# Grouping the depthwise tap rounds of layer 1: six groups of three in place of twelve groups of one or two

## What is computed

```
y = einsum(w_in (288x48), x)                      # 48 -> 288 channels
f = rfft2(8x8 patches of y) * fft_mask; y = irfft2(f)
y = conv 3x3 depthwise (288 channels, padding 1)  # nine taps
x1, x2 = split(y, 2)
out = einsum(w_out (48x144), gelu(x1) * x2);  x = x + out
```

## Time and profile before

| | before |
|---|---|
| median of three runs | 21097.66 us (21091.03 to 21103.62) |
| the profiled execution, own time | 21103.45 us |
| its span | 21101.9 us |
| PE busy, mean granted clock | 90%, 0.955 |
| DVE, ACT, POOL busy | 64%, 36%, 49% |

### The profile page before, as it was taken

The page is one execution under the profiler, slowest core; times in us unless marked ns, Lnnn a source line. Parts: engine busy times, 40 slices in busy tenths (PEclk is TensorE's granted clock), DMA queues, the critical chain, the costliest instruction groups (busy, mean ns, idle before and its releaser), DMA issues. The chain is left out here.

```text
span 21101.9 us, 501412 instructions
## 1 busy us (share of the span) xinstructions
PE 19033.5 (90%) x172464; PEld 11794.6 (56%) x172464; DVE 13401.1 (64%) x22319; ACT 7503.4 (36%) x22720; POOL 10333.9 (49%) x8692
## 2 busy tenths in 40 slices
PE   6998998989989989899899898999998989898999
PEld 4665455456655554566555445665555456565666
DVE  4444445656667776666677766666777667777744
ACT  3554232145542221455422214663222122222222
POOL 0000000067767740677677406886774078787810
PEclk9999999999999999999999999999999999999999
DMA  3231112655533336455333364553434666666633
GB/s 92 68 70 45 35 36 84 140 112 113 113 99 111 110 119 145 109 112 113 99 110 111 112 151 111 121 121 100 111 110 126 134 146 150 149 149 146 147 88 78
DMA packets 932423, 2318.18 MB, mean 110 GB/s; under 512 B 276340, under 2 KB 528504, under 8 KB 844124
## 3 DMA queue, kind: packets, MB, share of 16 engines
q1 hardware_dynamic: 500560, 1364.68, 27.8%
q0 software_dynamic: 430080, 928.96, 16.7%
HBM read 1915.53 MB, written 385.13 MB: 109 GB/s over the span
## 5 line engine op out<-in xcount | busy, mean ns | idle before, releaser
L1840 POOL DMA_INDIRECT e_got<-table,e_idx x6144 | 7479.2, 1217 | 2580.1 <-issue 1603.5
L1856 POOL DMA_INDIRECT e_got<-table,e_idx x2048 | 2553.1, 1247 | 691.6 <-issue 501.7
L1010 PE MATMUL b_p_conv<-b_z,b_diag 32*32 32x512 f32 x76032 | 2807.1, 599 | 3.3 <-issue 3.3
L530 PE MATMUL a_p_qk<-a_wst,a_stack 125*128 125x192 f32 x12288 | 2466.8, 337 | 230.9 <-ACT a_qh L661 214.0
L530 PEld LDWEIGHTS a_p_qk<-a_wst,a_stack 125*128 125x128 f32 x12288 | 2025.8, 191 | 670.5 <-issue 367.5
L1112 ACT ACTIVATE b_z<-b_p_z 128x256 f32<-128x256 f32 x2112 | 846.5, 401 | 4026.9 <-PE b_p_z L974 3608.2
L1894 DVE TENSOR_TENSOR e_got<-e_got,e_wt 128x1536 f32<-128x1536 f32 x1024 | 1778.6, 1752 | 684.9 <-DMA e_got<-table,e_idx 682.3
L1199 DVE TENSOR_TENSOR b_ym<-b_p_in,b_mask 128x512 f32<-128x512 f32 x1056 | 729.4, 691 | 1807.8 <-PE b_p_in L966 1807.6
L974 PEld LDWEIGHTS b_p_z<-const,b_ym 128*128 128x128 f32 x8448 | 1165.3, 198 | 1215.5 <-issue 713.3
L974 PE MATMUL b_p_z<-const,b_ym 128*128 128x128 f32 x8448 | 1541.1, 307 | 100.1 <-ACT b_z L1112 93.9
L2140 PE MATMUL d_p_v<-d_xs,d_ws 125*128 125x512 f32 x4608 | 1388.2, 449 | 64.0 <-issue 60.4
(11 more groups left out here) (291 smaller groups left out, 35444.6 us busy)
## 6 DMA issues: line engine op xcount, KB each, us to landing
e_got<-table,e_idx POOLq DMA_INDIRECT x8192
b_x<-planes SPq DMA_DIRECT2D x264, 395.1 KB
a_stack<-in_xp SPq DMA_DIRECT2D x256, 387.0 KB
c_stack<-planes SPq DMA_DIRECT2D x256, 387.0 KB
d_stack<-planes SPq DMA_DIRECT2D x512, 193.5 KB
table<-i_acc SPq DMA_DIRECT2D x256, 384.0 KB, 2.3
b_xr<-planes SPq DMA_DIRECT2D x264, 197.5 KB
planes<-b_out SPq DMA_DIRECT2D x264, 197.5 KB
```

Of the source, the lines that this page charges most:

```text
L530: m = pe.matmul(dst_, st[:, row, dx + 128 * t:dx + 128 * t + 128], wst[:, dx, 0:2 * C2], start=(dx == 0), stop=False)
L1010: mm = pe.matmul(p_conv[q // 2 * 2 + r % 2][BLK * c:BLK * (c + 1), :], diag[g][BLK * r:BLK * (r + 1), k, :], zs[BLK * r:BLK * (r + 1), g, ...
L1840: pool.indirect_dma_start(out=self.got[q][:, t, c * REC:(c + 1) * REC], out_offset=None, in_=self.flat, in_offset=bass.IndirectOffsetOnAxi ...
L1856: pool.indirect_dma_start(out=self.got[q][:, t, c * REC:(c + 1) * REC], out_offset=None, in_=self.flat, in_offset=bass.IndirectOffsetOnAxi ...
```

## The change

The eighteen rounds of a step stand in groups of three at slots 3, 5, 7 (g = 0) and 10, 12, 14 (g = 1). Before, they stood at slots 3 to 8 and 10 to 15 as 2, 1, 2, 1, 2, 1 for each g. No round, copy or product is added or taken away. `gelu(m, 0)` and `gates(m, ., 0)` stand one slot earlier. The number of beats per step stays at 16 from taps.

```diff
-    CONV = {3: (0, 0, 2), 4: (0, 2, 3), 5: (0, 3, 5), 6: (0, 5, 6), 7: (0, 6, 8), 8: (0, 8, 9),
-            10: (1, 0, 2), 11: (1, 2, 3), 12: (1, 3, 5), 13: (1, 5, 6), 14: (1, 6, 8), 15: (1, 8, 9)}
+    CONV = {3: (0, 0, 3), 5: (0, 3, 6), 7: (0, 6, 9), 10: (1, 0, 3), 12: (1, 3, 6), 14: (1, 6, 9)}
...
-                            taps(m, z[1 - par], *CONV[t], (2 if t in (3, 7, 10, 14) else 1) if half else 0)
+                            taps(m, z[1 - par], *CONV[t], (2 if t in (7, 14) else 3) if half else 0)
...
-                        if mid and t == 9:
+                        if mid and t == 8:
                             gelu(m, 0)
...
-                        if mid and t == 9:
+                        if mid and t == 8:
                             gates(m, 1 - par, 0)
```

## The result

The changed kernel takes **21507.36 us** (median of four runs, 21485.39 to 21514.08), the kernel before 21094.35 us in the same comparison (21084.56 to 21103.62). The ratio is 1.0193, with a 95% interval from 1.0178 to 1.0208: 413 us slower. The profiled execution has a span of 21499.5 us, 398 above that of before. 21500 was forecast.

What follows compares the result with a forecast made beforehand. PE was taken to bound layer 1, waits included. Steps without a jump at +3.5 us (19 an image) and with one at +2.7 (13) gave +406 us for four images, forecast 21500 us; own range 21400 to 21610, 8 in 10 21380 to 21660.

Steps and rivals of the forecast that it cites:

- The two waits: PE waits for ScalarE's `b_z` copy four times a step, 0.6 us each; `widen` for `xf` or `xp`, 0.4 to 0.6.
- even slots, `z` uncovered: Slots 4, 6, 8: without the single round, the next inverse waits for ScalarE's copy; +0.65 us each, +2.05 a step with gelu.
- odd slots, `xf` uncovered: Slots 11, 13, 15: without the single round, `widen` waits for ScalarE's `xf` copy; +0.55 us each, +1.65 a step.
- the jump: End of a loop iteration, thirteen steps an image: the `xf` wait vanishes in PE's idle time and `widen` starts earlier, -0.25 us.
- the rounds: Tap rounds on PE: six groups of three at 3.35 us replace six pairs and six singles, -0.2 us a step.
- The extra 0.1 for the moved gelu: Slot 8: `gelu(m, 0)` stands ahead of the copy on ScalarE and delays it, 0.1 us.
- three rounds are dear: Rival, chance 0.1: a group of three takes 3.53 us, +1.2 a step against the sum, +154, giving 21655 us.
- About 3.6 in place of 4.1: Loop jump: fewer us of "issue" per jump, counted as PE's idle time, about 3.6 in place of 4.1.
- Fewer switches: Rival, chance 0.05: with copies ready in time, each tap group removed saves up to 0.2 us; -179, giving 20920 us.
- Other things pay: Rival, chance 0.04: the jump's idle time shrinks far more and the half-clock stretch behind it vanishes; -286 against +406, 21220 us.
- The clock falls: Rival, chance 0.1: short idle pieces bring PE to 1.2 GHz more often in mid-step; +384, giving 21890 us.

Runs made afterwards that it cites:

- each half of the change: Kernel before with only the g = 0 rounds in threes: 21323.09 us; with only the g = 1 rounds in threes: 21273.66 us.
- `e4_early_spectrum`: Changed kernel with `turned` and `spectrum`, and their copies, ahead of `inverse` and its copy at slots 11, 13, 15: 21276.44 us, ratio to before 1.0095.
- `e11_even_early`: Changed kernel with g = 0 at slots 4, 6, 8, gelu and gates at 9, `turned` and `spectrum` ahead of `inverse` at slots 3, 5, 7, 11, 13, 15: 21079.65 us.
- `e12_before_early3`: Kernel before with `turned` and `spectrum` ahead of `inverse` at slot 3 alone: 20998.76 us, ratio to before 0.9958.
- `e9_last_round_back`: Changed kernel with the last g = 1 round back at slot 15, two left at slot 14: 21473.29 us, ratio to before 1.0181.

## Why the prediction was right

**What bounds, and what the change uncovers: shown.** The two waits appeared with the counts and lengths named, each half of the change brought one, and taking them away by order alone gave their price back (`e4_early_spectrum`, `e11_even_early`): in the steps with taps 191 and 365 of the 418 us. The forecast of 21500 stands against 21507, and +406 against +413.

**The terms, one by one.** I averaged the ways over all four images.

| term | forecast | measured |
|---|---|---|
| even slots, `z` uncovered | 128 x 2.05 = +262 | about +215 |
| odd slots, `xf` uncovered | 332 x 0.55 = +183 | 332 x 0.59 = +196 |
| the jump | 52 x -0.25 = -13 | 52 x -0.4 = -21 |
| the rounds | 128 x -0.2 = -26 | about +40 |
| sum | +406 | +430, layer 1 whole +417 |

(332 is three odd slots in 128 steps, less the 52 at a jump. The 13 us between the pieces and the whole I could not place.) That the forecast hit within 7 us is partly luck, since two errors mostly cancelled:

- *Even slots too dear by 47.* I took the distance of slots 2 to 3, 1.29 us, and not my own lower bound of 1.20, which is what slot 8 to 9 shows above. The extra 0.1 for the moved gelu was not there: the idle time behind slot 8 is 0.49 us, no more than at the other two. On ScalarE it starts 0.2 us after the taps' end (11052.13 against 11051.94), where the row of before had 0.62:

```profile
11052.13 1.09 ACT L1128 ACTIVATE b_ga<-b_p_conv 128x512 f32<-128x512 f32 x2 [3.30 <-PE b_p_conv L1009]
11053.37 0.40 ACT L1111 ACTIVATE b_z<-b_p_z 128x256 f32<-128x256 f32 x1 [0.16 <-PE b_p_z L973]
```

  The copy behind it then still waits 0.16 us for its inverse. Why the gelu of before started 0.62 us after the taps, I can't say.
- *The rounds too cheap by 66.* A group of three takes 3.34 us in the first image, as forecast (3.35). Beside the boxes it takes by slot 3.38 (slot 3), 3.49, 3.56, 3.57, 3.57 and 3.46 (slot 14), 3.46 over all images. That is inside the bounds of 3.23 to 3.53, more than half of the way to the rival "three rounds are dear". I took the price from nine rounds of the last strip, 9.68 us, a stretch at the layer's end that other work does not stand beside in the same way. Pairs had shown the same: 2.28 us without boxes, up to 2.49 with them.

By image this agrees: the first, where groups cost 3.34, lost 89 us, 2.8 for each of its 32 steps; the others 109, 3.4 a step.

**The jump: direction right.** PE's idle time shrank from 2.91, 3.25, 3.70 and 3.30 us by image to 2.60, 2.86, 3.31 and 2.74. "About 3.6 in place of 4.1" holds for the difference only; the row I had taken it from was one of the long ones.

**The rivals.** Fewer switches (20920 us): refuted. `e11_even_early` has six stays in the tap rounds a step fewer, 768 in all, and its copies are covered, yet its steps with taps last 53 us longer than before. Estimated from rows: 40 lost to the rounds, 5 x 128 x (1.05 - 0.97) = 51 lost to the longer way behind the taps, and 27 gained at slot 3, if that is worth what it was in `e12_before_early3`; these sum to +64. The 11 us that are left are 0.014 us for each stay shed, so each brought at most a few hundredths of a us. By the drain rule of the Trainium skill, page "TensorEngine Tiling (Array Packing)", section "Key Properties", each change of mode drains the array; the trace shows no more of a price than that. Other things pay (21220): the jump paid 21 us, not 286. The clock falls: it stayed, 0.96 to 0.97 in layer 1, 0.957 over all. But half clock in the first step, which the prediction took as given, hangs on the order: 0.52 in both kernels, up to 0.89 with the early spectrum. Dear rounds: partly true, 66 us of its 154.

## What to carry to other kernels

Before small pieces of work are gathered into larger ones on the bounding engine, ask which round trip to another engine each small piece covers. In an interleaved order, the gap that a piece fills is worth more than the cost of starting it: here 365 us that order alone gave back, against some 40 for the larger groups themselves. Where such a wait shows, first look for other work of the same slot that can be exchanged (here two short matmuls ahead of a third), since that moves no large piece. Compare stretch by stretch even where two whole times agree: `e11_even_early` equals the kernel before only because a gain in one stretch hides a loss in another. And take the price of a repeated piece from a stretch where the same neighbours run beside it.

## What the runs showed of the hardware

- Tap rounds of 32x32 tiles cost more while the boxes' gathers run: 3.34 us for three without them, 3.5 on average and up to 3.62 in the rows above with them. A pair is 2.28 us without them and 2.30 to 2.49 with them. Neither the places of the semaphores raised in them nor VectorE's products for the boxes explain it.
- The way PE, ScalarE's copy of 128x256, PE takes 1.20 to 1.29 us from the start of one product of two matmuls to that of the next, and the way through the smaller copies 0.92 us from the start of `spectrum`.
- The end of a loop iteration leaves PE idle for 2.6 to 3.7 us on average. It was 0.4 us less where the last tap round ahead of it was gone, and came back with that round (`e9_last_round_back`). A stretch at half clock stands behind 51 of the 52 jumps in the kernel before and behind all 52 in the changed one.
- The first step of layer 1, in which PE does short products and waits between them, ran at a mean clock of 0.52 in both kernels, and at 0.89 when `turned` and `spectrum` were put ahead of `inverse` at one slot of sixteen: 61 us less over the four images, from steps that the change itself doesn't touch. `widen` waits there at either clock, 0.41 us at half and 0.53 at full.
